# Attention scores of one batch in two groups of three units instead of three groups of two, with every engine's order rewritten for it

## The reference

```python
h = jnp.maximum(_layernorm(x, axis=-1), 0.0)
q, k, v = _heads(h @ Wq + bq), _heads(h @ Wk + bk), _heads(h @ Wv + bv)
scores = jnp.einsum('bhqd,bhkd->bhqk', q, k) / np.sqrt(HEAD_SIZE)
bias = jnp.where(adj, 0.0, NEG)[:, None]
probs = jax.nn.softmax(scores + bias, axis=-1)
ctx = jnp.einsum('bhqk,bhkd->bhqd', probs, v)
x = x + (merge_heads(ctx) @ Wf + bf)
```

## Time and profile before

| | before |
|---|---|
| median of 3 runs | 590.62 us (589.86 to 590.72) |
| profiled execution, its time | 591.8 us |
| its span, first to last instruction | 590.0 us |
| mean granted clock | 0.996 |
| PE busy | 573.5 us (97%) |
| PE weight loads | 428.9 us (73%) |
| ACT busy | 516.1 us (87%) |
| POOL busy | 491.3 us (83%) |
| DVE busy | 473.8 us (80%) |
| DMA queue of SP | 79.6% of 16 engines' span |

### The profile page before, as it was taken

One profiled execution on the slowest core, in us unless ns is written; L12 is line 12 of the kernel. 1 busy time (PEld: TensorE's weight loads), 2 busy tenths in 40 slices (PEclk: granted clock), 3 DMA queues, 4 the chain that ended last, 5 costly groups with the idle time before them and its releaser, 6 DMA issues.

```text
span 590.0 us, 17760 instructions
## 1 busy us (share of the span) xinstructions
PE 573.5 (97%) x6640; PEld 428.9 (73%) x6640; DVE 473.8 (80%) x1484; ACT 516.1 (87%) x1161; POOL 491.3 (83%) x533
## 2 busy tenths in 40 slices
PE   7997999999999999999999999999999999999977
PEld 7676777777777777777777777777777777777755
DVE  4988788888888888878888887887877778787775
ACT  1788999899999999999999999999999999999882
POOL 2779998888998888899888889988888988888960
PEclk9999999999999999999999999999999999999999
DMA  8047889788888978899988877899988788987584
GB/s 273 10 77 140 133 169 184 158 169 167 156 156 165 176 162 168 174 129 174 179 167 170 162 169 150 158 183 156 183 162 159 151 159 181 160 157 143 72 162 117
DMA packets 275641, 92.01 MB, mean 156 GB/s; under 512 B 257634, under 2 KB 275555, under 8 KB 275555
## 3 DMA queue, kind: packets, MB, share of 16 engines
q1 hardware_dynamic: 274352, 90.87, 79.6%
q10 hardware_dynamic: 1202, 0.01, 0.1%
HBM read 17.05 MB, written 12.58 MB: 50 GB/s over the span
## 4 chain that ended last, share of the span: by engine, by line
PE 80%; DVE 6%; ACT 5%; DMA 5%; issue 2%; POOL 2%; ACTq 0%; SPq 0%; DVEq 0%; POOLq 0%
PE ring L1106 18%; PE ring L1108 18%; PE ring L1107 18%; PE scores L1169 11%; PE ctx L1195 5%; PE ring L1207 3%; PE ctx L1197 3%; PE ctx L1196 3%; DMA p_cols<-p_rows 3%; ACT probs L574 2%; DVE logits L796 1%; DVE h_rows L813 1%; DMA bf_row<-in_L_gnn_bf_dram 1%; ACT qk L602 1%; POOL p_rows L440 1%
## 5 line engine op out<-in xcount | busy, mean ns | idle before, releaser
L440 POOL TENSOR_TENSOR p_rows<-probs,p_rows 128x512 f16<-128x512 f32 x190 | 220.6, 1161 | 30.2 <-ACT p_rows L582 29.8
L796 DVE CUSTOM_DVE_ANT_0 logits<-scores,mask,logit_unscale 128x256 f32<-128x256 f32 x384 | 169.1, 478 | 57.5 <-PE scores L1169 57.3
L574 ACT ACTIVATE probs<-logits,raised 128x256 f32<-128x256 f32 x372 | 168.9, 501 | 6.1
L1106 PE MATMUL ring<-h_cols,w_hi 128*128 128x256 f16 x576 | 157.2, 273 | 0.0
L1108 PE MATMUL ring<-h_cols,w_lo 128*128 128x256 f16 x576 | 157.0, 273 | 0.0
L1107 PE MATMUL ring<-h_cols,w_hi 128*128 128x256 f16 x576 | 156.9, 272 | 0.0
L426 POOL TENSOR_TENSOR split<-qk,split 128x512 f16<-128x512 f32 x96 | 111.4, 1160 | 36.4 <-DVE split L820 36.4
L582 ACT ACTIVATE p_rows<-probs 128x512 f16<-128x512 f32 x190 | 119.6, 630 | 5.9
L602 ACT ACTIVATE qk<-ring,qk_bias_s,qkv_ratio 128x256 f32<-128x256 f32 x192 | 96.5, 552 | 3.9 <-PE ring L1108 3.8
L1195 PEld LDWEIGHTS ctx<-v_hi,p_cols 128*128 128x128 f16 x756 | 69.0, 97 | 33.9 <-issue 26.1
L1195 PE MATMUL ctx<-v_hi,p_cols 128*128 128x65 f16 x756 | 88.1, 195 | 5.5 <-DMA p_cols<-p_rows 4.1
(11 more groups left out here) (116 smaller groups left out, 1155.7 us busy)
## 6 DMA issues: line engine op xcount, KB each, us to landing
x_in<-in_x_dram SPq DMA_DIRECT2D x32, 384.0 KB, 3.8
out_dram<-result SPq DMA_DIRECT2D x62, 192.0 KB, 2.2
p_cols<-p_rows SPq DMA_TRANSPOSE x190, 3.2
adj_in<-in_adj_dram SPq DMA_DIRECT2D x32, 64.0 KB, 2.6
w_raw<-in_L_gnn_Wq_dram SPq DMA_DIRECT2D x1, 576.0 KB, 6.1
w_raw<-in_L_gnn_Wv_dram SPq DMA_DIRECT2D x1, 576.0 KB, 7.9
w_raw<-in_L_gnn_Wf_dram SPq DMA_DIRECT2D x1, 576.0 KB, 9.0
h_cols<-h_rows SPq DMA_TRANSPOSE x29, 4.8
```

The lines of the kernel that those rows point to most:

```text
L440: pool.tensor_tensor(p_rows[u][:, 1], probs[u % 3][:], p_rows[u][:, 0], ALU.subtract).then_inc(p_lo_ready, 1)
L574: act.activation(probs[u % 3][:, a], logits[u % 3][:, a], ACT.Exp, bias=raised[u % 3][:, a:a + 1], scale=-1.0).then_inc(probs_ready, 1)
L796: dve.tensor_tensor_reduce(out=logits[u % 3][:, a], in0=score_bank[a][:, u % 2 * S:(u % 2 + 1) * S], in1=mask[b.parity][:, t], scale=logit ...
L1106: pe.matmul(out_ap, a_hi, m_hi, start=first, stop=False)
```

## The change

One batch's six units are scored in two groups of three (units 0 to 2, units 3 to 5). The bank of the peaks becomes a third score bank, and `score_of` lays the six halves of a group over three banks. The first group needs all three pairs of q and k of its batch before it starts. In bank 1 the last head of the group (unit 2, head 1) follows the first (unit 0, head 0) in another half of the array; a new semaphore `shared_bank_done` makes it wait for that. Batch 0 is scored in four groups, (0, 1), (2), (3), (4, 5). The order on every engine is written anew.

```diff
-        score_bank = [bank("scores0"), bank("scores1")]
-        peak_bank = bank("peaks")
+        score_bank = [bank(f"scores{n}") for n in range(3)]
+        peak_bank = score_bank[2]
...
+        def score_of(u, a):
+            n, column = ((1, 0), (2, 0), (0, 0), (2, S), (0, S), (1, S))[u % C * 2 + a]
+            return score_bank[n][:, column:column + S]
...
-            def scores(b, g):
-                for u in (2 * g, 2 * g + 1):
+            def scores(b, units):
+                for u in units:
                     if u < C:
                         wait(pe, qk_hi_ready, b.count(C, u + 1))
                         wait(pe, qk_lo_ready, b.count(C, u + 1))
-                wait(pe, logits_ready, b.count(2 * UNITS, 4 * g))
+                wait(pe, logits_ready, b.count(2 * UNITS, 2 * units[0]))
...
                         for a in range(2):
+                            if u % C == 2 and n == 0 and a == 1:
+                                wait(pe, shared_bank_done, b.count(GROUPS, u // C + 1))
...
+                            if u % C == 0 and n == 2 and a == 0:
+                                mm.then_inc(shared_bank_done, 1)
...
             def cycle(b):
+                scores(b, (0, 1, 2))
+                apply_probs(b + -1, 2)
                 if (b + -2).exists():
                     project_out(b + -2, 1)
+                project_qk(b + 1, 0)
+                apply_probs(b + -1, 3)
+                apply_probs(b + -1, 4)
+                transpose_context(b + -1, 0)
+                scores(b, (3, 4, 5))
+                project_qk(b + 1, 1)
+                apply_probs(b + -1, 5)
+                project_qk(b + 1, 2)
+                project_out(b + -1, 0)
+                apply_probs(b, 0)
+                project_v(b + 1, 0, (0,))
+                apply_probs(b, 1)
+                project_v(b + 1, 0, (1, 2))
+                transpose_context(b + -1, 1)
+                project_v(b + 1, 1)
```

More of the change, by code:

```diff
@@ L60, in gnn_attention @@
     UNITS = QT * C
[L61 removed]
+    GROUPS = UNITS // C
     LAG = 4
@@ L262, in pair, with scored @@
             return slice(j * P, (j + 1) * P)
+        def scored(b, u):
+            if b.k == 0:
+                return (1, 1, 2, 3, 4, 4)[u]
+            return 4 + (b.k - 1) * GROUPS + u // C + 1
         def w_scale(n):
@@ L267, in gnn_attention, with cycles @@
         BY_PE = 3
-        def cycles(cycle):
-            for k in range(1, B - 2):
+        def cycles(cycle, first=1):
+            for k in range(first, B - 2):
                 cycle(Batch(k))
@@ L673, in cycle @@
             def cycle(b):
[L674 to L713, removed]
+                v_hi_part(b, 1)
+                exps(b, 0)
+                exps(b, 1)
+                probs_hi(b, 0)
+                probs_hi(b, 1)
+                context_hi(b + -1, 0)
+                qk_full(b + 1, 0)
+                exps(b, 2)
+                probs_hi(b, 2)
+                h_hi_rows(b + 2)
+                qk_full(b + 1, 1)
+                exps(b, 3)
+                probs_hi(b, 3)
+                qk_full(b + 1, 2)
+                exps(b, 4)
+                context_hi(b + -1, 1)
+                probs_hi(b, 4)
+                exps(b, 5)
+                v_hi_part(b + 1, 0)
+                probs_hi(b, 5)
             cycles(cycle)
@@ L788, in mask_and_max @@
                 t, j = u // C, u % C
-                wait(dve, scores_ready, b.count(GROUPS, u // 2 + 1))
+                wait(dve, scores_ready, scored(b, u))
                 if u == 0:
@@ new lines, in _ @@
+            apply_probs(Batch(0), 2)
+            project_qk(Batch(2), 0)
+            apply_probs(Batch(0), 3)
+            project_qk(Batch(2), 1)
+            apply_probs(Batch(0), 4)
+            transpose_context(Batch(0), 0)
+            scores(Batch(1), (3, 4, 5))
+            apply_probs(Batch(0), 5)
+            project_qk(Batch(2), 2)
+            apply_probs(Batch(1), 0)
+            pe.wait_ge(w_lo_ready, 8)
+            project_out(Batch(0), 0)
+            project_v(Batch(2), 0, (0,))
@@ L1319, in cycle @@
-                if front:
-                    project_v(b + 1, 0, (1, 2))
-                    project_v(b + 1, 1)
-            cycles(cycle)
+                project_qk(b + 1, 0)
[7 more added lines that the diff above has]
+                project_out(b + -1, 0)
@@ L1325, in turn_probs @@
+                apply_probs(b, 0)
[4 more added lines that the diff above has]
+                project_v(b + 1, 1)
+            cycles(cycle, 2)
             def turn_probs(u):
```

323 lines of the change are left out of this document (133 added, 190 removed).

## The result

The changed kernel takes **599.89 us** (median of 4 runs, 599.0 to 601.23), the kernel before 590.55 (4 runs, 589.86 to 590.72): ratio 1.0157, 95% interval 1.0134 to 1.0179. It is slower by 9 us; the prediction said 8 us faster.

A forecast was written before the change was run, and what follows sets the result against it. The prediction took PE's product-to-product distances as the bound. Savings of 5.7 (group edges), 0.5 (short waits) and 1.5 (tail), 7.7 us in all, took 590.6 to 582.9 us, range 579.5 to 588.5.

The forecast's parts named there:

- The edges of the groups: PE's entry and exit of each score group: 0.19 us lost per group, 30 fewer groups, 5.7 us saved.
- the group of 18: Score group of 18 products on PE: 1.09 us to the next product.
- its place in the cycle: Second group on PE starts 6.06 us after the first, in a cycle of 17.02.
- (d): New wait inside a group, at the seventh pair on PE: met by 0.01 us, cost 0, at most 6.8.
- The tail: Batch 31 drains one group less: 1.5 us gained, bounds a loss of 1.5 and a gain of 3.2.
- The rival that the change does nothing: Edge loss comes from a wait, so fewer groups give nothing: 590 us; chance 0.08 together with the missed wait.
- (e): Chain from PE's transposes through ACT, DVE and POOL to pair 2's low part: done 16.49, needed 17.02, cost nothing.
- short waits: Short PE waits in the old cycle, 0.07 us each: 0 to 2.0 us may go, 0.5 taken.
- The collision rival: CASTs collide with POOL: chain grows by 1.12 us, 29 cycles lose 17, 600 us; chance 0.10.
- (a): Logits on DVE: unit 2 read by 4.8 us, second group needs it at 6.06; cost nothing, cover 1.2.
- (b): Transposed probabilities: unit 4 tightest, landed at 3.9 us, needed at 5.24; cost nothing, cover 1.3.
- (f): Ramp and tail: ramp 0 with bounds of 1.5 us either way, tail a gain of 1.5.

The follow-up runs named there:

- x9: x8 with both parts of h moved ahead of pair 0 on ACT and DVE; 584.33 us, ratio 0.9877 to the kernel before.
- x10: x6 with the logits of unit 5 ahead of pair 2's CAST on DVE; 586.62 us, ratio 0.9916 to the kernel before.
- x3: Changed kernel with two PE waits ahead of the first group instead of five, the logits' wait first; 595.88 us, ratio 1.007 to the kernel before.
- x6: Changed kernel with POOL's residual add cut to one column in batches 3 to 28, order unchanged; 597.31 us, ratio 1.0093 to the kernel before.
- x2: Changed kernel with POOL's residual of the next batch moved from ahead of pair 1 to the cycle's end; 603.07 us, ratio 1.0186.
- x1: Changed kernel with the CAST of pair 1 ahead of the low part of h on DVE; 614.4 us, ratio 1.0377 to the kernel before.
- x8: Changed kernel with x3 and x4 together, plus pair 0's bias ahead of the high part of the context on ACT; 590.78 us, ratio 0.9988.
- x4: Changed kernel with the statistics of batch b + 3 behind v's low parts on DVE; 597.77 us, ratio 1.0101 to the kernel before.

## Why the prediction was wrong, point by point

**The gain was there.** The edges of the groups, the group of 18, its place in the cycle and the wait inside the group (d) came out as worked out: no hole in the group and 17.00 to 17.03 per cycle wherever PE waits for nothing (x9, x10). The tail gave 1.7 for 1.5: its two long waits (2.0 and 1.2) are gone and shorter ones came. The rival that the change does nothing is refuted by x9, and by x10.

**The step that failed is (e).** It named the right chain and the right order, and put its spare time at 0.53 us. Measured on the chain, the low part of h took 1.92 for 1.35 (+0.57), the probabilities of unit 3 1.30 for 1.11 (+0.19), and PE began 0.24 behind the release where the sum took it as at once; 0.1 of that goes with the wait that stands behind the releasing one (x3, x6). Together 1.0, less the 0.53, is the 0.47 by which the cycle is too long. In 28 cycles that is 13 us, and the late probabilities add 2.2. The sum for the profiled execution, 584.1, still held 2.8 us in these cycles above 17.02 each (it took 0.5 off for short waits and kept the rest), so of the 15 us between it and the 599.0 some 12.5 lie in the cycles and 2.2 in the start.

The row behind the 1.35 was itself a partly blocked pair: one of its two instructions took its free time, as both do in x2 and x6 with 1.01 together, and the other did not. A duration taken from one row of the old order carries the neighbours that it had there. The new order puts POOL's residual beside both. The prediction looked for such neighbours at the CASTs alone. x6 shows that this is the term: without the residual the pair takes 1.01, and the low part of pair 2 ends 16.46 behind the first group, where the prediction had 16.49.

**The collision rival** had the mechanism, with the wrong instruction: the CAST of pair 1 took its free 0.41, and that of pair 2 was blocked (1.28), but ended (309.44) a microsecond before POOL came to it (310.41). That its 600 us hit the time is luck: its 1.12 of delay was near to the 1.0 that other terms made. The Trainium skill has the rule for the low part of h (SBUF — State Buffer, section "Who interferes with whom"): a DVE instruction with two SBUF inputs contends with a GpSimd instruction that reads SBUF. The traces agree: 1.01 us beside an idle POOL (x2, x6), 1.84 to 2.79 beside a busy one (the changed kernel, x1, x8, x9). The prediction used that section's rule for casts and not this one.

**(a) was incomplete.** It priced the logits that the second group waits for, not those of unit 5, for which the next first group waits and which stood behind pair 2's CAST and the moments. In x1 and x6 it is what PE waits for, with cycles of 18.12 and 17.51; in the changed kernel it was 0.22 short of that.

**(b)** put the cost of the transposed probabilities at nothing. It was 1.7 us: 2.2 us in single long cycles, all at unit 4, which (b) named as the tightest, against 0.5 before.

**(f), the start,** was 0 with bounds of 1.5 and came out as a loss of 2.2, which x4 takes away whole: the change had put statistics that wait for a load ahead of v's low parts, and the prediction did not look at what they wait for that early.

## What to carry to other kernels

Before a reorder is priced from old durations, list for each instruction of DVE and POOL on the tightest chain what the other of the two will be doing beside it in the new order, and take the free and the held-up duration as its two bounds; a cover of 0.5 us on a chain of fifteen steps over four engines is no cover. Where a wait vanishes, ask which chain is next and what the edit does to it: here the second was 0.22 us behind the first, and opening the first alone (x6) made it later and gave nothing per cycle. What can be held up is best put into time in which its own engine idles ahead of a wait (x9).

## What was not expected of the hardware

- The blocking reaches tiny instructions: the variance of two columns (TENSOR_SCALAR, 128x2) took 0.85 to 1.07 us beside POOL's work, and 0.17 free.
- It goes both ways: POOL's 1.16 became 1.34 to 1.48 beside such DVE instructions (x1 shows 1.47 beside the low part of h, and 1.48 beside its end and the CAST of pair 2).
- A wait that stands behind the one that releases PE goes with about 0.1 us: 0.25 from the release to the product in the changed kernel, where the logits' wait follows the releasing one; 0.15 in x3 and 0.14 in x6, where the releasing one is the last (x6 has all the waits). In x10, where the release comes earlier, they cost nothing.
